# Loading the second layer's values from GpSimd's queue in place of SP's (attention and expert layers, one core of Trainium2)

## The reference

```
x = x + L0_xattn(layernorm(x), ctx)          # 16 heads of 8
x = x + L0_ffn(layernorm(x))                 # 8 experts, the best 2 of each row, mixed by a softmax of two
x = x + L1_xattn(layernorm(x), ctx, mask)    # 16 heads of 64
x = x + L1_ffn(layernorm(x))                 # 128 -> 512 -> 128, relu
```

```
kv = context @ Wkv; k, v = split(kv); q = x @ Wq            # (32, 16 heads, 128, 64)
dots = q k^T * 64**-0.5 - (1 - mask)[:, None, :, None] * 1e6
out = softmax(dots) v;  return concat(out) @ Wout + bout
```

## Time and profile before

| | us |
|---|---|
| median of 3 runs | 915.78 (908.65 to 916.70) |
| the profiled execution, its own time | 913.91 |
| its span, first to last instruction | 912.3 |
| TensorE busy in the span | 828.5 (91%) |
| ACT busy | 673.3 (74%) |
| DVE busy | 638.7 (70%) |
| GpSimd busy | 453.2 (50%) |
| TensorE's share in the chain that ended last | 67% |
| transfers' share in that chain | 9% |

### The profile page before, as it was taken

How to read it: one execution, slowest core, us unless ns; L and a number is a source line. 1 busy time by engine, 2 the same in 40 slices (tenths; PEclk the granted TensorE clock), 3 DMA queues, 4 the chain that set the end, 5 groups by cost and what they waited for, 6 DMA issues and landing times.

```text
span 912.3 us, 28139 instructions
## 1 busy us (share of the span) xinstructions
PE 828.5 (91%) x7885; PEld 734.4 (80%) x7885; DVE 638.7 (70%) x2052; ACT 673.3 (74%) x2662; POOL 453.2 (50%) x765
## 2 busy tenths in 40 slices
PE   5899999999998877999999678999999999999985
PEld 3677777777776766999999577889999999999974
DVE  5888887887887743222222578788898888888872
ACT  2999899899898852333334798899888888888860
POOL 3135445444454362111113777788777777776540
PEclk9999999999999997999999899999999999999987
DMA  5897667667767702222222198889899999999871
GB/s 169 247 244 217 204 208 227 201 211 228 219 208 240 196 30 78 70 71 70 70 70 64 64 253 253 253 240 269 246 241 232 238 238 237 240 239 240 240 233 41
DMA packets 160451, 171.93 MB, mean 188 GB/s; under 512 B 16052, under 2 KB 139318, under 8 KB 160374
## 3 DMA queue, kind: packets, MB, share of 16 engines
q1 hardware_dynamic: 153474, 156.77, 60.0%
q0 software_dynamic: 6112, 13.90, 5.7%
q10 hardware_dynamic: 788, 0.39, 0.2%
HBM read 90.87 MB, written 80.13 MB: 187 GB/s over the span
## 4 chain that ended last, share of the span: by engine, by line
PE 67%; DMA 9%; issue 8%; DVE 6%; SPq 4%; POOL 3%; ACT 3%; another core or an unknown queue 0%; POOLq 0%; DVEq 0%; ACTq 0%
PE bank L1233 8%; PE bank L1420 8%; PE bank L1392 7%; PE bank L1399 7%; PE bank L1442 5%; PE bank L1516 4%; PE bank L1432 4%; PE bank L1225 4%; DMA PTC<-turned_blocks 3%; PE bank L1506 3%; PE bank L1187 3%; PE bank L1344 3%; PE bank L1304 2%; PE bank L1521 2%; ACT PR L699 2%
## 5 line engine op out<-in xcount | busy, mean ns | idle before, releaser
L699 ACT ACTIVATE PR<-PR,nmx 128x128 f32<-128x128 f32 x512 | 198.4, 393 | 13.7 <-DVE nmx L898 13.6
L699 ACT ACTIVATE PR<-bank,nmx 128x128 f32<-128x128 f32 x512 | 188.0, 432 | 0.4 <-DVE nmx L898 0.4
L347 POOL TENSOR_TENSOR PR<-PR,rden 128x512 f32<-128x512 f32 x128 | 133.1, 1052 | 50.4 <-DVE rden L903 49.8
L699 ACT ACTIVATION_READ_ACCUMULATOR PR<-bank,nmx 128x1 f32 x512 | 139.6, 273 | 0.0
L1420 PE MATMUL bank<-XCT,wqk 128*128 128x128 f32 x832 | 104.6, 280 | 10.0 <-ACT XCT L687 9.7
L793 ACT ACTIVATE H<-bank 128x512 f32<-128x512 f32 x70 | 41.8, 597 | 92.3 <-PE bank L1392 92.3
L1420 PEld LDWEIGHTS bank<-XCT,wqk 128*128 128x128 f32 x832 | 98.3, 193 | 13.5 <-ACT XCT L687 10.5
L699 ACT ACTIVATION_READ_ACCUMULATOR PR<-PR,nmx 128x1 f32 x512 | 98.2, 192 | 0.0
L1187 PEld LDWEIGHTS bank<-ident,PR 128*128 128x128 f32 x512 | 60.2, 141 | 39.6 <-issue 38.1
L1065 DVE STREAM_TRANSPOSE BT<-PR 128x512 f32<-128x512 f32 x128 | 89.7, 701 | 2.3 <-POOL PR L347 1.5
L898 DVE TENSOR_REDUCE nmx<-bank 128x4 f32<-128x512 f32 x128 | 86.2, 673 | 4.5 <-PE bank L1225 3.5
(11 more groups left out here) (186 smaller groups left out, 1986.1 us busy)
## 6 DMA issues: line engine op xcount, KB each, us to landing
turned_blocks<-BT SPq DMA_DIRECT2D x64, 512.0 KB
PTC<-turned_blocks SPq DMA_DIRECT2D x256, 128.0 KB, 4.2
second_layer_values<-wide SPq DMA_DIRECT2D x32, 512.0 KB
wide<-second_layer_values SPq DMA_DIRECT2D x32, 512.0 KB
expert_outputs<-HF SPq DMA_DIRECT2D x32, 256.0 KB
expert_outputs<-HF SPq DMA_DIRECT2D x64, 128.0 KB
KBD<-expert_outputs SPq DMA_DIRECT2D x64, 128.0 KB
QS<-expert_outputs SPq DMA_DIRECT2D x32, 256.0 KB
```

What stands on the lines that cost most here:

```text
L347: nc.gpsimd.tensor_tensor(unit, unit, rden[:, p, G * g:G * g + G].unsqueeze(2).broadcast_to([P, G, P]), ALU.mult).then_inc(s["nm"], 1)
L699: last = nc.scalar.activation(PR[:, g, j * P:(j + 1) * P], scored, ACT.Exp, bias=nmx[:, p, h:h + 1], accum_out=den[:, p, h:h + 1])
```

## The change

Three pieces. SP's step no longer loads the values: the wait for `pv` and the load are gone from between the output store and the store of the next half of blocks. GpSimd's step gets both, right behind unit 3's scale, one step later in its count (it loads n - 1 in step n, into the same buffer as before). And GpSimd waits once, ahead of the second layer, for the first stage's 32 stores of values.

```
@@ SP, step1 @@
                     sp.dma_start(out[n - 3], acc[:, q, :]).then_inc(out_stored[q], 16)
                 if exists(n):
-                    wait(sp, c["pv"], NU * (n - 1))
-                    sp.dma_start(V1[:, p, :, :].rearrange("p h d -> p (h d)"), v_dram[n]).then_inc(c[f"v{p}"], 16)
                     store_blocks(n, p, 0)
@@ GpSimd, ahead of step1, and step1 @@
             pool.wait_ge(ld_ffn, 27 * 16)
+            pool.wait_ge(a["vst"], 16 * NB)
             wait_apart(pool, (b["st"], total * 16))
...
                 if exists(n - 2):
                     scale_pool(pool, c, n - 2, p, 3)
+                if exists(n - 1):
+                    wait(pool, c["pv"], NU * (n - 2))
+                    pool.dma_start(V1[:, q, :, :].rearrange("p h d -> p (h d)"), v_dram[n - 1]).then_inc(c[f"v{q}"], 16)
                 if exists(n + 1):
                     wait_apart(pool, (c["xn"], n + 2))
```

## The result

| | before | after |
|---|---|---|
| median of 3 runs, us | 915.78 (908.65 to 916.70) | 948.41 (943.52 to 951.51) |
| span of the profiled execution | 912.3 | 949.7 |
| mean granted clock of TensorE | 0.974 | 0.973 |

The changed kernel takes 1.0373 times as long, 95% interval 1.0266 to 1.048. The forecast was 928 (912 to 940), slower with a chance of 0.70. The direction was right, the size was not: 32.6 us more by the medians, where 12 were forecast.

The account below looks back on a forecast made before the run. TensorE was taken to bound the kernel. From the profiled 913.9 us, +16.8 in the loop, -2 before it, -1 in the first sequences and -1 after it gave 926.7, so a median of about 928, range 912 to 940.

Parts of the forecast that it names:

- The shift on GpSimd: In the register loop, 1.1 us of wait and 1.30 of issue start the bias behind unit 3's scale 2.4 later.
- The slack: GpSimd's spare time before TensorE waits in a loop step: 0.64 us ahead of need plus 0.74 idle, 1.38.
- The long steps: Steps at a lowered TensorE clock, in the loop; priced only in a rival, one or two at 1.7 us each.
- The relief ahead of the loop: Before the loop, freeing SP's queue gains at most 6.6 us against 4.4 of GpSimd cost: net -2 us.
- the loads only change places: Before the loop, GpSimd's loads get no cheaper, only move, so nearly all the 4.4 us cost was taken.
- the 6.6 of the working: Most that SP's queue could give back before the loop: 4.9 us of waits plus 1.7 of lowered clock.
- Wait and issue on GpSimd: Before the loop, 0.55 us a step over some eight steps, 4.4 us.
- The rival of no relief: Before the loop, TensorE's waits stay at 4.9 us and only GpSimd's 4.4 are added: 935; chance 0.12.
- the rival with contention: In the loop, the values' load delays turned blocks, 0.5 us more a step, plus lowered-clock steps: 939; chance 0.12.
- After the loop: GpSimd's DMA costs nothing there; of 4.5 us of TensorE's waits for turned blocks, 1 is won.

Follow-up runs that it names:

- the wait alone: The kernel before plus one GpSimd wait behind unit 3's scale for TensorE's last values product, with no load moved; ratio 1.0058.
- the end of the step: The changed kernel with GpSimd's load of the values moved to the end of its step, behind unit 2's scale; ratio 1.0037 to the kernel before.
- the small load: The changed kernel with GpSimd's load, after the first two sequences, cut to 8 KB in place of 512; ratio 1.0238 to the kernel before.

## Why the prediction was wrong in size

- **The shift on GpSimd, 2.4 us: right.** Measured 2.46, with 1.05 of wait and 1.41 of issue for the 1.1 and 1.30 of the working.
- **The slack, 1.38 us: too large, the first step that failed.** I counted the 0.64 us between `rstd` and L330 as free. But DVE can't start at the moment at which `rstd` ends: in the changed kernel, where it waits for nothing else, L330 (790.98) starts 0.34 behind `rstd` (790.07 + 0.57). The slack was 0.74 + 0.64 - 0.34 = 1.04. Then 2.46 - 1.04 = 1.42 is due, where 1.35 and 1.19 are measured, and for the wait alone 1.41 - 1.04 = 0.37, where 0.44 and 0.20 are measured. Sixteen steps at a mean of 1.27 make 20.3 us, not 16.8.
- **The long steps: not in the sum.** 7.4 us in this trace. The table of stretches showed it beforehand: a step of 13.75 at a clock of 0.88 behind a gap of 1.86 us. I priced it only for a rival. Where a gap grows to a microsecond and more in sixteen steps, a few such steps belong in the sum, or at least in the upper end of the range.
- **The relief ahead of the loop, 2 us net: the wrong sign, and the largest error.** Measured 10.5 more in the nine steps and 1.8 by the first values product, so 12.3 where 3 less were forecast. The failed step is the sentence that the loads only change places. Their place in the queue protected the turned blocks: on SP's queue the loads were issued behind these, and put ahead of them on the same queue they raised TensorE's waits from 5.1 to 11.1 us on chip E. The removal of the 512 KB altogether gives 4.6 us here (101.3 to 96.8), so a relief was there to be had, a little less than the 6.6 of the working. Wait and issue on GpSimd, for which the working has 4.4, come to 2.1 without the bytes (98.8 against 96.8). With the bytes another 13.0 come on top (111.8 against 98.8), and for these the working has nothing: -4.6 + 2.1 + 13.0 is the 10.5 measured, each term from one trace. The 1.8 by the first values product weren't looked into. The rival of no relief was nearer, but priced this at zero too; the rival with contention named the mechanism and looked for it in the loop, where the turned blocks have the slack of a longer step. TensorE waits 1.3 us for them there in all.
- The rule in the Trainium skill, page DMA: Bandwidth & Descriptors, section Issuing engines are not separate DMA queues, says that transfers of all issuing engines interleave on the same 16 DMA engines. By that rule no time is won, and the traces agree. They show more, a loss of 10.5 us in nine steps with the share of these engines as before (0.88 and 0.87). Their median landing, 3.4 us before and 6.0 after, fits blocks that were not interleaved with the loads before and are now.
- **After the loop, 1 us: 3.0 measured.** Right in sign.

Sum: 16.8 - 2 - 1 - 1 = 12.8 us of the working against 1.8 + 10.5 + 28.1 - 3.0 = 37.4 of the trace. Of the 24.6 between them 15.3 are the part ahead of the loop, 11.3 the loop (3.5 the slack, 7.8 the long steps and what lies in single ones), and 2.0 come back after it.

No kernel of this study beats the one before by more than can be told. The best that does all the work is the load behind the next store on SP's queue, 0.9989 (0.9953 to 1.0025).

## What to carry to other kernels

A transfer's place in its queue worked here like a priority: put ahead of the turned blocks on the same queue, the loads made TensorE wait 11.1 us for these and not 5.1. Before you move one to another queue, ask what it stood behind, whether that is on the critical path, and how busy the transfer engines are then: at a share near 0.9 the time of issue counted here, and the end of the step cost 4 us where the start cost 12. On an in-order engine, add what you insert between the event you wait for and the result that the bound engine needs, and subtract only the idle time that is really there, less the handover to the next engine (0.34 us here). And when a change opens a gap in TensorE's work each step, let the range reach to a few steps at the lower clock.

## What the runs showed of the hardware

- A DMA of 128 rows with a wait and a register address costs GpSimd 1.41 us behind what it waited for (0.66 of it in its row). With 8 KB in place of 512 its row is 0.66 long too, and the regular steps are the same (13.19 and 13.59): the price is the issue's, not the bytes'.
- The load took about as many microseconds of transfer engines on ScalarE's queue as on GpSimd's: 13.4% of 16 x 109.2 us against 19.1% of 16 x 111.2 less the gathers' 5.7% of 16 x 100.4, which is 234 against 248 us for 4.7 MB. So no sign that the same bytes occupy the transfer engines longer from GpSimd's queue.
- Behind a gap of 2.0 us (the small load's step at 740.93) and one of 2.48 (the changed kernel's at 808.36) TensorE ran at its lower level for the next groups (1.67 and 2.08 us for eight matmuls of the projections, where 1.16 is usual); behind one of 2.65 us (the small load's step at 796.33), one of 2.5 on chip C, and behind all the regular ones of 1.4 to 1.8, it did not.
- Chips differ by 3.7% on the same kernel (medians of 882 and 915 us), but a step whose length GpSimd's program sets took 13.20 us on two of them alike.
